# A fused two-layer block on one core: attention started during the normalization, expert work spread over all attention steps, and the mixing of layer 0 moved behind them

## The reference

```
xn = layernorm(x)
s  = window_attention(xn)              # 16 heads, windows of 64 rows, relative bias, projection
g  = silu(xn + gate * expert(xn))      # top-1 of 32 experts, at most 160 rows each, hidden size 256
x  = x + s * g
xn = layernorm(x)
s  = fft_binding_attention(xn)         # q, k, v projections, unit spectra, running sum, unbinding
g  = silu(sum of top-2 of 8 experts)   # hidden size 1024, gelu
out = x + s * g
```

## Time and profile before

| what | value |
|---|---|
| median of three runs | 1414.13 us (1413.33 to 1418.07) |
| the profiled execution | 1420.41 us, its span 1418.3 us |
| PE busy | 1142.8 us (81% of the span) |
| DVE busy | 667.3 us (47%) |
| ACT busy | 535.8 us (38%) |
| POOL busy | 451.5 us (32%) |
| granted TensorE clock, mean | 0.878 of full speed |

### The profile page before, as it was taken

The page is one execution under the profiler, slowest core; times in us unless marked ns, Lnnn a source line. Parts: engine busy times, 40 slices in busy tenths (PEclk is TensorE's granted clock), DMA queues, the critical chain, the costliest instruction groups (busy, mean ns, idle before and its releaser), DMA issues.

```text
span 1418.3 us, 16237 instructions
## 1 busy us (share of the span) xinstructions
PE 1142.8 (81%) x6014; PEld 975.0 (69%) x6014; DVE 667.3 (47%) x1380; ACT 535.8 (38%) x1051; POOL 451.5 (32%) x438
## 2 busy tenths in 40 slices
PE   4741589999999466575568999999999999999940
PEld 3731468888887355453467888888888888888930
DVE  5260556666665576675556655655661000000027
ACT  1210353434333244342404556555642323232444
POOL 1007434343434645532142322232222223231300
PEclk8765699999999677786757999999999999999975
DMA  9002214444442522110140424433444588464956
GB/s 341 12 20 96 74 56 139 146 138 136 149 133 89 160 68 76 60 45 15 58 190 23 157 108 163 171 116 141 168 171 178 224 298 321 163 222 160 331 166 207
DMA packets 97087, 201.75 MB, mean 142 GB/s; under 512 B 9871, under 2 KB 82065, under 8 KB 92017
## 3 DMA queue, kind: packets, MB, share of 16 engines
q1 hardware_dynamic: 83264, 164.17, 33.0%
q0 software_dynamic: 13744, 36.55, 7.2%
HBM read 160.08 MB, written 41.55 MB: 142 GB/s over the span
## 4 chain that ended last, share of the span: by engine, by line
PE 61%; DVE 10%; issue 7%; ACT 5%; DMA 4%; POOL 3%; SPq 2%; POOLq 0%; ACTq 0%
PE PS L1018 15%; PE PS L1008 14%; PE PS L947 5%; PE PS L906 5%; PE PS L849 3%; PE PS L919 2%; PE PS L827 2%; PE PS L916 2%; PE PS L970 2%; PE PS L873 2%; PE PS L884 2%; PE PS L859 2%; PE PS L836 1%; ACT L1764 1%; SPq L1958 1%
## 5 line engine op out<-in xcount | busy, mean ns | idle before, releaser
L1008 PE MATMUL PS<-xgT,WE 128*128 128x256 f32 (+1 forms) x1248 | 261.2, 366 | 7.7 <-ACT hT L1764 5.8
L1018 PE MATMUL PS<-WE,hT 128*128 128x256 f32 x1136 | 251.6, 379 | 0.0
L1008 PEld LDWEIGHTS PS<-xgT,WE 128*128 128x128 f32 x1248 | 221.3, 193 | 40.8 <-ACT hT L1764 11.9
L1018 PEld LDWEIGHTS PS<-WE,hT 128*128 128x128 f32 x1136 | 213.8, 190 | 28.0
L1764 ACT ACTIVATE hT<-PS,WE 128x256 f32<-128x256 f32 (+1 forms) x312 | 138.4, 454 | 236.4 <-PE PS L1008 221.8
L1549 DVE TENSOR_TENSOR y<-PS,WE 128x512 f32<-128x512 f32 (+1 forms) x39 | 25.1, 644 | 396.9 <-PE PS L1018 396.9
L1877 POOL DMA_INDIRECT result<-y,result_of x71 | 70.9, 999 | 296.4 <-DVE y L1549 277.1
L1801 POOL TENSOR_TENSOR sc<-sc,sc_max 128x512 f32<-128x512 f32 x64 | 68.8, 1076 | 128.4 <-DVE sc_max L1208 128.0
L1806 POOL TENSOR_TENSOR prob<-prob,row_sum 128x512 f32<-128x512 f32 x64 | 68.7, 1074 | 93.5 <-DVE row_sum L1215 92.1
L849 PE MATMUL PS<-KB,Q 128*128 128x256 f32 x256 | 76.9, 429 | 24.8 <-DVE KB L1182 13.4
L947 PE MATMUL PS<-XT,Wf 128*128 128x256 f32 x384 | 88.4, 388 | 3.4 <-DMA Wf<-wf_dram 2.8
(11 more groups left out here) (226 smaller groups left out, 1835.6 us busy)
## 6 DMA issues: line engine op xcount, KB each, us to landing
WE<-in_experts SPq DMA_DIRECT2D x39, 2180.0 KB
X<-in_x SPq DMA_DIRECT2D x16, 512.0 KB
wgt<-in_w_gate SPq DMA_DIRECT2D x32, 256.0 KB, 2.7
wgt<-in_w_up SPq DMA_DIRECT2D x32, 256.0 KB, 3.0
wgt<-in_w_down SPq DMA_DIRECT2D x32, 256.0 KB, 2.7
both<-result SPq DMA_DIRECT2D x16, 512.0 KB, 8.7
table<-zeros POOLq DMA_DIRECT2D x1, 5120.0 KB, 19.7
rows<-table SPq DMA_DIRECT2D x40, 128.0 KB
```

What stands on the lines that cost most here:

```text
L1008: m = e.matmul(PS[:, FIRST_H_BANK + nth % HR, 0:rows], W1[n % WR][:, k, c * P:(c + 1) * P], xgT[:, n % 2, k, 0:rows], start=k == 0, stop=k ...
L1018: m = e.matmul(PS[:, u.bank, j * D:(j + 1) * D], hT[:, n % 2, c, j * P:(j + 1) * P], W2[n % WR][:, c, :], start=c == 0, stop=c == KF - 1)
```

## The change

The start is written out as one list: groups of statistics, normalization and transposes are overlapped, q, k and v of unit 0 come after the first group's transposes, and the first scores follow the last router logits and `fold`. The routing is a generator of its own beside the first attention steps, and its 32 scatters go in eight pieces of four, one piece a step in steps 1 to 8. In the first ten steps DVE subtracts the maximum itself, so that POOL has only the share to do. The 69 pieces of expert work are spread over the half steps from step 11 to step 62. The combination follows when all steps are planned, quarter by quarter with its stages staggered over three iterations, four buffers of gathered rows, and layer 1's normalization and router in groups of four tiles. The experts' buffers are moved away from `X`, which is not loaded again. In layer 1 the square roots of two chunks stand together in every second slot.

```diff
-UNITS, UW, UT, SR, PR0, STEPS = NT // 2, 4, 2 * P, 2, 4, 2 * NT
+UNITS, UW, UT, SR, PR0, STEPS = NT // 2, 4, 2 * P, 2, 5, 2 * NT
-FIRST_TILES = 8
-FIRST_EXPERT_STEP = 7
+EARLY_STEPS, FIRST_EXPERT_STEP, LAST_EXPERT_STEP = 10, 11, 62
+PUT_TILES, GOT = 4, 4
+EXPERT_PIECES = GT + 2 * E0
...
     def start():
+        add("stats", 0, 0)
+        add("stats", 0, 8)
+        add("norm", 0, 0)
+        turn(0, 0)
+        add("q_bias")
+        add("stats", 0, 16)
+        add("norm", 0, 8)
+        q(0)
+        k(0)
+        v(0)
+        turn(0, 8)
+        add("stats", 0, 24)
+        add("norm", 0, 16)
+        logits0(0)
+        logits0(8)
+        turn(0, 16)
+        add("norm", 0, 24)
+        logits0(16)
+        turn(0, 24)
+        logits0(24)
         for g in range(0, NT, 8):
...
+            need(("logits0_out", g))
         add("route0_best")
+        fold()
+
+    def routing():
+        add("route0_hot")
         yield
         route0_count()
         yield
+        add("route0_running")
+        yield
         add("route0_put")
+        add("route0_rows", 0)
         yield
         add("route0_get")
         yield
-        add("route0_gate")
-        yield
+        for t in range(PUT_TILES, NT, PUT_TILES):
+            add("route0_rows", t)
+            yield
+            if t == 2 * PUT_TILES:
+                add("route0_gate")
+            yield
...
     def combination():
-        add("x_again")
...
+        for q in range(GOT):
+            add("mix_gather", q)
+        for i in range(QUARTERS + 3):
+            if i < QUARTERS:
+                add("mix_gate", i)
+            if 0 <= i - 1 < QUARTERS:
+                add("mix_silu", i - 1)
+                if i - 1 + GOT < QUARTERS:
+                    add("mix_gather", i - 1 + GOT)
+            if 0 <= i - 2 < QUARTERS:
+                add("mix_add", i - 2)
+                add("stats", 1, 4 * (i - 2))
+            if i >= 3:
+                g = 4 * (i - 3)
                 add("norm", 1, g)
+                turn(1, g, 4)
                 route1(g)
...
+    def side(half):
+        if advance(route):
+            wanted = (half - 2 * FIRST_EXPERT_STEP + 1) * EXPERT_PIECES // (2 * (LAST_EXPERT_STEP - FIRST_EXPERT_STEP))
+            while pieces[0] < min(wanted, EXPERT_PIECES + 1):
+                advance(ffn)
+                pieces[0] += 1
+
+    start()
     score(0)
     score(1)
     for s in range(STEPS + 4):
...
+    combination()
...
-        if ch + 1 < CHUNKS:
-            add("magnitudes", ch + 1)
+        if n % 2 == 0:
+            for later in (ch + 1, ch + 2):
+                if later < CHUNKS:
+                    add("magnitudes", later)
...
                 e.tensor_reduce(sc_max[:, r, :], by_head, AX.X, ALU.max).then_inc(sc_max_done, 1)
+                if s < EARLY_STEPS:
+                    w.wait_ge(sc_max_done, s + 1)
+                    e.tensor_tensor(by_head, by_head, sc_max[:, r, :].unsqueeze(2).to_broadcast([P, PAIRS, WIN]),
+                                    ALU.subtract).then_inc(early_sub_done, 1)
...
-            if what == "route0_put":
+            if what == "route0_rows":
                 w.wait_ge(put_ready, 1)
                 w.wait_ge(ln_xn, NT)
                 w.wait_ge(table0_zeroed, 16)
-                for t in range(NT):
+                for t in range(at[0], at[0] + PUT_TILES):
...
-            elif what == "mix_add":
+            elif what == "mix_silu":
                 q, = at
                 w.wait_ge(silu_ready, q + 1)
...
+                e.tensor_tensor(S[:, 4 * q:4 * q + 4, :], got0[:, q % GOT, :, :], S[:, 4 * q:4 * q + 4, :], ALU.mult).then_inc(
                     scaled0, 1)
...
             elif what == "load0_first":
+                w.wait_ge(gate_ready, 1)
                 w.wait_ge(scattered0, 16 * NT)
-                w.wait_ge(ln_xn, NT)
...
-            elif what == "x_again":
-                for i in range(2):
-                    w.wait_ge(y0_out[i], 16 * E0)
-                for q in range(QUARTERS):
-                    e.dma_start(X[:, 4 * q:4 * q + 4, :], x_view[:, 4 * q:4 * q + 4, :]).then_inc(x_in[q], 16)
```

More of the change, by code:

```diff
@@ L221, in down, with turn @@
         order.product("down", ex, columns=8 * D, frees=2, then=[("y_out", 100)])
-    def turn(layer, g):
-        for t in range(g, g + 8, 2):
+    def turn(layer, g, tiles=8):
+        for t in range(g, g + tiles, 2):
             order.take(("turn", layer, t // 2), (4, 5)[(t // 2) % 2])
@@ L291, in experts, with advance @@
                     add("load_down", ex + 1)
-                yield
+            yield
         down(E0 - 1)
-        yield
-    projected = set()
     def combination():
-        add("x_again")
-        add("mix_gather", 0)
-        add("mix_gather", 1)
-        yield
-        for q in range(QUARTERS):
[L304 to L318, removed]
+        for q in range(GOT):
[12 more added lines that the diff above has]
+                g = 4 * (i - 3)
                 add("norm", 1, g)
-                yield
-                turn(1, g)
-                yield
+                turn(1, g, 4)
                 route1(g)
[L324 to L343, removed]
+    def advance(generator):
+        return next(generator, generator) is generator
+    route, ffn, pieces = routing(), experts(), [0]
+    def side(half):
[5 more added lines that the diff above has]
+    start()
     score(0)
@@ L356, in schedule0 @@
             proj((s - 3) // 2)
-            projected.add((s - 3) // 2)
-        side(s)
+        side(2 * s + 1)
         if s < STEPS:
             pturn(s)
-    for _ in combine:
-        pass
+    assert next(ffn, None) is None and next(route, None) is None
+    order.settle(order.clock + STEPS * UT)
+    combination()
     order.settle(order.clock + STEPS * UT)
@@ L754, in turn @@
             w.wait_ge(const_in, 16)
-            for pair in range(g // 2, g // 2 + 4):
+            for pair in range(g // 2, g // 2 + (2 if layer else 4)):
                 u = use["turn", layer, pair]
@@ L1028, in filled_by, with group_of @@
             w.wait_ge(full[u.bank], u.filled)
+        def group_of(layer, g):
+            return ((4, NT // 8 + g // 4 + 1) if layer else (8, g // 8 + 1))
         def stats_of(layer, g):
-            for t in range(g, g + 8):
+            n, nth = group_of(layer, g)
+            for t in range(g, g + n):
                 if layer == 0:
@@ L1290, in vector @@
                 e.memset(nyq_reset[:, :].rearrange("p (b t) -> p b t", b=BATCH)[:, :, 0:1], 0.0).then_inc(nyq_reset_ready, 1)
-                last = use["route1", NT - 8]
-                w.wait_ge(free[last.bank], last.emptied)
+                for g in range(0, NT, 4):
+                    last = use["route1", g]
+                    w.wait_ge(free[last.bank], last.emptied)
                 w.wait_ge(bf_done, 1)
@@ L1704, in scalar @@
                 w.wait_ge(mixed0, q + 1)
-                w.wait_ge(silu_ready, q)
-                w.wait_ge(wf_saved, 16)
-                w.wait_ge(full[3], use["vp",].filled)
-                e.activation(mix_tanh[:, :, :], got0[:, q % 2, :, :], ACT.Tanh, bias=0.0, scale=0.5).then_inc(gated0, 1)
-            elif what == "route1":
+                last = use["pturn", STEPS - 1]
+                w.wait_ge(full[last.bank], last.filled)
+                w.wait_ge(silu_ready, q - 1)
+                e.activation(mix_tanh[:, q % 2, :, :], got0[:, q % GOT, :, :], ACT.Tanh, bias=0.0, scale=0.5).then_inc(gated0, 1)
+            elif what == "route1_out":
                 g, = at
@@ L1824, in gpsimd @@
                 q, = at
+                i = q % GOT
                 w.wait_ge(get_ready, 1)
-                for i in range(2):
-                    w.wait_ge(y0_out[i], 16 * E0)
-                if q < 2:
-                    w.wait_ge(table0_zeroed, 16)
+                for n in range(2):
+                    w.wait_ge(y0_out[n], 16 * E0)
+                if q < GOT:
+                    last = use["score", STEPS - 1]
+                    w.wait_ge(full[last.bank], last.filled)
                 else:
-                    w.wait_ge(x1_ready, q - 1)
+                    w.wait_ge(scaled0, q - GOT + 1)
                 for j in range(4):
```

161 lines of the change are left out of this document (81 added, 80 removed).

## The result

The changed kernel takes **1334.95 us** (median of 4 runs, 1332.12 to 1335.51) beside 1416.1 us for the kernel before on the same chip (4 runs, 1413.33 to 1420.62): ratio **0.942** [0.9389, 0.9451]. The forecast was 1321 us, 1300 to 1350. The profiled execution took 1335.51 us, with a span of 1333.7. One run of this study (the sixth of e1, 1432.71 us at a mean granted clock of 0.81, where the other five have 0.89 to 0.90) was in a slower state and is left out of every comparison.

A forecast was written before the change was run, and what follows sets the result against it. Layer 0's stages left TensorE idle except the long one, where it was full; filling them gives 71 + 96 + 331 + 87 + 7 = 592 us to the first spectrum, with layer 1 at -3, hence 1321 us, range 1300 to 1350.

The forecast's parts named there:

- Start: Up to the first attention score: 71 us instead of 95.85, range 66 to 78.
- the low value: Router logits in the start: 3.88 us a group at the low end, 6.88 at the high; taken nearer 3.88.
- Steps to the first gather: Attention steps before the mixing: 96 us for steps 0 to 10, then 331 us for steps 11 to 63.
- the rival of 8.8 us a step between scatters: Steps 1 to 8, beside the scatters, run at 8.8 us each, making the stage 21 us longer: 1342; chance 0.12.
- The prices of 3.6 us for a step and 4.4 for an expert: Long stage, steps 11 to 63: TensorE needs 3.6 us per attention step and 4.4 us per expert.
- the slower rival: Long stage: one step's own chain, not TensorE, sets 8.8 us a step, 466 us instead of 331: 1456; chance 0.04.
- Mixing: Combination of expert rows after all attention steps, now bare: 87 us, lower bound 80.
- the rival of the two engines: Mixing: VectorE and GpSimd exclude each other, adding 16 us on silus and some 5 on gates: 1342; chance 0.18.
- Last norm to first spectrum: From the mixing's last norm to layer 1: 7 us instead of 8.5, set by the load of Wf.
- Layer 1: From first spectrum to the end, 736 us before: -3 us, between 0 and -5.
- The term of the tables: Layer 1: half as many loads of gelu's table in 15 slots, -3 us.
- The scale: Conversion of the profiled 1327 us to the runs' median: 6.3 us taken off, giving 1321.

The follow-up runs named there:

- e1: Changed kernel with the first ten steps' subtraction of the maximum put back from VectorE to GpSimd; 1337.31 us against 1334.95.
- e3: Changed kernel with all 32 scatters issued in one block instead of eight pieces between early steps; 1357.86 us against 1334.95.
- e2: Changed kernel with experts packed one to each step from step 11 to 46, the last steps holding attention alone; 1350.07 us against 1334.95.
- e6: Changed kernel with the mixing's quarters run in a row, not staggered; 1387.32 us against 1334.95.
- e4: Changed kernel with layer 1's square roots taken one chunk a slot again, not two every other slot; 1338.56 us against 1334.95.
- e8: Changed kernel with layer 1's routing scores moved ahead of the first spectra on every engine; 1329.75 us against 1334.95.
- e10: Changed kernel with 20 unused matmuls added on TensorE, five ahead of the transposes of each of tile pairs 4 to 7; 1333.54 us against 1334.95.
- e5: Changed kernel with the mixing's multiplication of gated rows moved from GpSimd to VectorE; 1331.12 us against 1334.95.
- e9: Changed kernel with the load of Wf issued ahead of the mixing's stores of normalized rows; 1335.04 us against 1334.95.

## Why the prediction was right, and where its terms were off

The mechanism was as told where a run tested it (e1's stage set by GpSimd, the pieces by e3, the spreading by e2, the stagger by e6, the table loads by e4). The span came out 8.7 us above the forecast's 1325: the five terms below were off by +7.1, -2.1, +4.0, +1.4 and -1.8 us. That the whole is within about 1% is in part luck, since errors cancelled between the terms and within the first and the third.

- **Start, 78.1 us instead of 71: mis-sized by 7.** I took the logits nearer the low value, because a busy stretch has the high clock. TensorE fell to 0.50 in the gaps before them, and the first two groups took 13.7 us where I had 2 x 3.88. So my reason failed: a stretch without a gap ran 13.7 us at the low clock. By the earlier trace rows both values were there to be seen; my bounds, 67.5 to 79.5, held them both, and the range that I gave stopped at 78, just short. The rest of the stage was off both ways: q, k and v took 5.5 us where I had 9.2, `fold` 14.3 where I had 12, and three waits of 2.1, 2.4 and 1.5 us (at 27.54, 31.34 and 58.98) were not in the sum, which had TensorE never waiting from 28.6 on. The later groups are a toss: the second logits took 3.8 to 4.04 us in nine profiles of this study and 6.87 or 6.88 in four (e2, e3, e8, e10), of which only e10 changes anything ahead of them; this is the 4 to 5 us by which first scores differ in the table.
- **Steps to the first gather, 424.9 us instead of 427.** First scatter 36.4 us after the first score (38), scatters and shares 52 us (49), that is 6.5 us a step: the rival of 8.8 us a step between scatters was wrong. TensorE was full in the long stage at the clock 1.00. The prices of 3.6 us for a step and 4.4 for an expert held: from step 11's exponential, at 168.7, to the last, at 493.4, it is 6.24 us a step, where I had 6.2. e2 shows that the slower rival (steps bound by their own chain) had the wrong cause. The first gather waited 2.2 us for the last experts' store, which I hadn't seen.
- **Mixing, 91.0 us to the end of the last norm instead of 87: mis-sized by 4.** First addition 23.8 us after the first gather (24). From there to the last norm's end 67.2 us instead of 63.5, with VectorE busy for 62 of them, so nearly full as told. Its work came out as summed only because two errors cancelled: the silus, which I had at 1.86 us, weren't stretched once (mean 1218 ns, 5.2 us less in all), and the norms took 5.8 us more than I had. Norms and gates were stretched, up to 3.1 and 3.3 us for one tile, and two additions waited 3.3 us each. So the rival of the two engines was in part right: 8.1 us of stretch, by e5, instead of its 21, and in other instructions. The Trainium skill (SBUF — State Buffer, "SBUF: two separate sides") names, beside two-input operations, VectorE's perf modes as holders of the lock; the norm, an operation with one tensor as its input that went from 0.40 us to 3.13 beside a multiplication of 2.36, agrees. In which mode it runs no trace shows, and the recorded starts don't tell who held what: the norm's is at 551.23, ahead of the multiplication's at 551.84, and it is the norm that was drawn out. I had counted only the two-input ones.
- **Last norm to first spectrum, 8.4 us instead of 7, for another reason.** I gave the load of `Wf` as the cause. e9 shows that it isn't it: TensorE works without a gap from 583 to 602.5 at 0.50, 5.3 us a quarter, and is behind.
- **Layer 1, 731.2 us instead of 733.** The term of the tables is 2 to 3 us by e4, as 14 loads at the 0.2 us of the earlier trace rows would give (2.8); the rest of the 4.8 us against the kernel before, some 2 us, wasn't taken apart.
- **The scale.** I took off 6.3 us, because the profiled execution of before stood that far above its median. That of the changed kernel stands 0.6 above its own. 5.7 us of the miss of 14 (1334.95 against 1321) are from this step: one execution's distance from the median isn't a property to carry over.

## What to carry to other kernels

Put a block of one engine's work (here 32 scatters) beside the first steps of the stage that it doesn't feed, and cut it so that the steps' own items on that engine come between the pieces; the price of each side, read from a full stretch of the trace, held here (6.24 us a step where I had 6.2, 52 us of scatters and shares where I had 49). When a stage becomes bare, look at its chain across engines (a stagger was worth 51 us of 150) and at operations on VectorE that stand beside GpSimd's: handing one over to the idle engine can cost more than it saves. Look for items of the critical chain that wait in a queue behind work nobody needs yet: moving one item gave 5.5 us.

## What was not expected of the hardware

- TensorE at 0.50 while busy without a gap: 33 to 47 us, 583 to 604 us, and 641 to 668 us of the changed kernel; it was at 0.50 already in the gaps ahead of each. With the gaps ahead of the first filled (e10) it held 1.00 for 8 us longer and then fell within a stretch without gaps, so gaps alone don't account for it; what does is open.
- The same order of work gave the second logits 3.8 to 4.0 us in some executions and 6.9 in others.
- A scatter or gather issued by GpSimd took 1.0 us alone, and up to 1.8 and 3.45 us beside VectorE's operations with two inputs; with the ten early subtractions off VectorE (e1) the scatters took 0.97 to 1.06 us.
